# The mixture stages of a four-layer kernel: a tile's down products behind the next tile's up products, rows gathered seven tiles ahead

## The chip, the cores and the metric

The kernel runs on one core of one Trainium2 chip, as one program and one launch. The metric is the time of one execution on the device in microseconds (us); the median of three runs is compared. TensorE is called PE in the profile, VectorE DVE, ScalarE ACT, GpSimd POOL and SyncE SP.

## The reference

The input `x` is 4 sequences of 512 rows of 512 floats (2,048 tokens). Four steps follow one another, each added to `x`: a small cross attention, a feed-forward block 0 (self attention, then a mixture of experts), a second cross attention with a mask, and a feed-forward block 1 (a mixture only). The two mixtures are what the change touches:

```python
# block 0: 1 shared expert and 7 routed ones, inner width 256, each token takes 2
h = silu(x @ wg) * (x @ wu) / 8.0
out = h @ wd                      # summed over the chosen experts with their weights
# block 1: 32 routed experts, inner width 192, each token takes 8
h = silu(x @ wg[e]) * (x @ wu[e])
acc = acc + (h @ wd[e]) * w_e[:, None]
```

## The kernel before, in words

All matmuls are float32 in accuracy. The large ones are made of three products in the faster format fp32r: a factor is split into a high part (rounded) and a low part (the rest), and high by high, high by low and low by high are summed.

The function `mixture` runs once for each mixture. The (token, expert) pairs are sorted by expert into tiles of 128 rows; every tile has one expert. Mixture 0 has 56 tiles (the first 16 are those of the shared expert, whose rows come in order by plain DMA), mixture 1 has 160. The tiles are unrolled in groups of 8 (`GROUP`): the first group or groups as straight code, then a hardware loop, then the last group. The engines each run their own list and meet at semaphores; nothing plans the order but the order in which the lines stand. For tile t:

- POOL gathers the 128 rows of the tile from HBM with an indirect DMA (`gather`, L1462) into one of 8 buffers, 6 tiles ahead (`AHEAD`), and later adds the tile's 128 result rows into one of two sums in HBM (`add`, L1478, an indirect DMA that adds). One `gather(t + AHEAD)` and one `add(t)` alternate. An `add` waits for the tile's result, and for the `add` of two tiles before to have landed, since that one wrote the same sum. In mixture 0's shared tiles `keep` (L1469) stands for `add`.
- PE turns the rows (`flip`, L1739, four 128x128 transposes). ACT copies the turned rows to their high part (`flip` of ACT, L1507), DVE makes the low part (`rows_rest`, L1648).
- ACT and DVE split the expert's weights 4 and 3 tiles ahead: ACT the high part of the up weights (`split`, L1524) and of the last rows of the down weights (`tail_of_weights`, L1540), DVE the low parts (`split_rest`, L1654; `tail_rest`, L1668, or `part_rest` L1661 in mixture 0).
- PE runs the up products (`up`, L1758 to L1760, 12 matmuls of 384 columns in mixture 1, of 512 in mixture 0).
- ACT takes the silu (`silu`, L1546), DVE multiplies (`product`, L1676 and L1677) and so makes `hid`.
- PE turns `hid` (L1774, two transposes, called the hidden flip below). ACT (`tail_of_hidden` L1534, `half_of_hidden` L1529) and DVE (`flip` of DVE, L1639 and L1642, or L1636 and L1637) copy it out.
- PE runs the down products (L1784, a float32 matmul that the trace shows as two, then L1789 and L1790, or L1792 to L1794).
- ACT scales the result by the row's weight into one of 4 buffers (L1574), and POOL adds it.

The order of PE in a turn of the loop for tile t is: hidden flip of t, `flip` of t + 2, `up` of t + 1, down products of t. That of ACT: `tail_of_hidden(t)`, `flip(t + 2)`, `expert_of` and `tail_of_weights(t + 4)`, `silu(t + 1)`, `split(t + 4)`, result of t. That of DVE: `flip(t)`, `place_of(t + 3)`, `rows_rest(t + 2)`, `tail_rest(t + 3)`, `product(t + 1)`, `split_rest(t + 3)`.

`expert_of` and `place_of` read a tile's expert from a table in SBUF into a register of the engine, which then forms addresses with it:

```python
needed = act.value_load(of_tile[0:1, 1, bass.ds(t, 1)], min_val=1, max_val=E)
```

SP loads the weights of the experts into a ring of 4, waiting until the down products of the expert four before are done. `listing` turns the table of row numbers once, at the start of a mixture.

## Time and profile before

| what | value |
| --- | --- |
| median of 3 runs (lowest, highest) | 1813.72 us (1808.09, 1817.69) |
| span of the profiled execution, first to last instruction | 1822.5 us |
| PE busy | 1582.2 us, 87% |
| PE weight loads | 1206.6 us, 66% |
| DVE busy | 1399.5 us, 77% |
| ACT busy | 1082.6 us, 59% |
| POOL busy | 789.0 us, 43% |
| the core's granted TensorE clock, mean | 0.913 |

The span is the profiled execution's own time; no other time was taken of that execution. It is 8.8 us (0.5%) above the median of the runs. Mixture 0 lies between about 599 and 907 us, mixture 1 between about 1067 and 1789 us. An engine's busy time is the union of its instructions. Matmuls are pipelined and their ends are modelled, so PE can show no gap and yet wait a little: the starts of its instructions tell more than its idle time.

### The profile page before, as it was taken

The page shows a single profiled execution, that of the slowest core. Times are in us where ns is not written, and L with a number is a line of the kernel's source. Part 1 is how long each engine was busy: PE and PEld are TensorE (multiplying, and loading weights), DVE is VectorE, ACT ScalarE, POOL GpSimd, SP SyncE. Part 2 cuts the span into 40 slices and gives each one's busy share as a digit, 9 for nine tenths or more (in the row PEclk, how much of TensorE's full clock was granted, in tenths as well). Part 3 has the DMA queues.
Part 4 walks back from the last instruction along what each step waited for, and adds up shares of the span by engine and source line. Part 5 has one row for each costly group of instructions (what it writes and reads, how often), then busy time and mean ns, then how long its engine had stood idle before and what let it go on. Part 6 is the DMA issues. An engine that isn't in the chain of part 4 may idle for free. (4 is left out here: it accounts for less than half of the span.)

```text
span 1822.5 us, 34829 instructions
## 1 busy us (share of the span) xinstructions
PE 1582.2 (87%) x8910; PEld 1206.6 (66%) x8911; DVE 1399.5 (77%) x2889; ACT 1082.6 (59%) x2081; POOL 789.0 (43%) x547
## 2 busy tenths in 40 slices
PE   4578899898887799999779929999999999999991
PEld 2546667666565577777546517887878787887880
DVE  6836866767674588888567858998989998998992
ACT  1124634546352477888433317888878887888870
POOL 5100010110302324555301135788878877778881
PEclk9588998999998799999976658999999999999995
DMA  9225436453521635865564415878788888997778
GB/s 338 80 69 133 101 82 150 89 140 74 124 63 47 203 101 135 210 107 107 74 216 139 154 35 132 210 155 202 156 209 170 176 189 198 223 227 164 131 123 301
DMA packets 169999, 270.58 MB, mean 148 GB/s; under 512 B 20416, under 2 KB 96192, under 8 KB 168192
## 3 DMA queue, kind: packets, MB, share of 16 engines
q0 software_dynamic: 49008, 117.24, 32.6%
q1 hardware_dynamic: 120896, 152.18, 28.4%
q8 instruction: 46, 0.75, 0.2%
q14 instruction: 49, 0.40, 0.1%
HBM read 153.72 MB, written 89.06 MB: 133 GB/s over the span
## 5 line engine op out<-in xcount | busy, mean ns | idle before, releaser
L1654 DVE TENSOR_TENSOR moe_w_lo<-moe_w_up,moe_w_hi 128x1536 fp32r<-128x1536 f32 (+1 forms) x216 | 408.6, 1892 | 1.7 <-ACT moe_w_hi L1524 1.7
L1524 ACT ACTIVATE moe_w_hi<-moe_w_up 128x1536 fp32r (+3 forms) x216 | 343.2, 1589 | 0.0
L1462 POOL DMA_INDIRECT moe_rows<-moe_rows,moe_ids x200 | 308.4, 1542 | 67.2 <-issue 57.3
L1758 PE MATMUL psum<-moe_w_hi,moe_rows_hi 128*128 128x384 f32 (+1 forms) x864 | 324.2, 375 | 4.8 <-DVE moe_rows_lo L1648 4.8
L1759 PE MATMUL psum<-moe_w_lo,moe_rows_hi 128*128 128x384 f32 (+1 forms) x864 | 305.5, 354 | 0.0
L1760 PE MATMUL psum<-moe_w_hi,moe_rows_lo 128*128 128x384 f32 (+1 forms) x864 | 305.5, 354 | 0.0
L1784 PE MATMUL psum<-moe_w_down,moe_hid_t 128*128 (+1 forms) x432 | 221.0, 593 | 2.7 <-DVE moe_hid_lo L1637 1.4
L1478 POOL DMA_INDIRECT moe_sum<-moe_res,moe_ids x100 | 172.0, 1720 | 98.3 <-ACT moe_res L1574 49.2
L1478 POOL DMA_INDIRECT moe_other<-moe_res,moe_ids x100 | 172.3, 1723 | 91.7 <-ACT moe_res L1574 30.0
L1648 DVE TENSOR_TENSOR moe_rows_lo<-psum,moe_rows_hi 128x512 fp32r<-128x512 f32 x216 | 149.3, 691 | 69.2 <-issue 53.4
L739 ACT ACTIVATE prob<-psum,neg_top 128x128 f32<-128x128 f32 (+3 forms) x256 | 133.3, 528 | 83.1 <-DVE neg_top L869 78.5
L1758 PEld LDWEIGHTS psum<-moe_w_hi,moe_rows_hi 128*128 128x128 f32 x864 | 165.0, 191 | 13.2 <-DVE moe_rows_lo L1648 5.8
L1760 PEld LDWEIGHTS psum<-moe_w_hi,moe_rows_lo 128*128 128x128 f32 x864 | 164.4, 190 | 9.9
L1759 PEld LDWEIGHTS psum<-moe_w_lo,moe_rows_hi 128*128 128x128 f32 x864 | 165.4, 191 | 7.6
L869 DVE TENSOR_REDUCE neg_top<-psum 128x1 f32<-128x128 f32 (+3 forms) x256 | 117.6, 484 | 50.0 <-PE psum L1093 49.7
L1507 ACT ACTIVATE moe_rows_hi<-psum 128x512 fp32r<-128x512 f32 x216 | 130.6, 605 | 28.5 <-PE psum L1739 28.2
L1739 PE MATMUL psum<-const_sb,moe_rows 128*128 128x128 f32 x864 | 132.1, 276 | 14.1 <-DMA moe_rows<-moe_rows,moe_ids 12.6
L1546 ACT ACTIVATE moe_gate<-psum 128x192 f32<-128x192 f32 (+1 forms) x216 | 74.0, 342 | 110.4 <-PE psum L1760 108.9
L1540 ACT ACTIVATE moe_tail_hi<-moe_w_down 128x512 fp32r (+1 forms) x160 | 101.1, 632 | 61.3 <-issue 57.6
L1134 PE MATMUL psum<-const_sb,prob 128*128 128x128 f32 x640 | 111.3, 290 | 29.8 <-ACT prob L739 26.6
L1789 PE MATMUL psum<-moe_tail_hi,moe_tail_t 128*128 128x512 f32 x160 | 127.2, 795 | 0.0
L293 POOL DMA_INDIRECT moe_slots<-entry,slot x24 | 23.9, 994 | 232.1 <-DVE slot L992 225.6
(295 smaller groups left out, 3121.2 us busy)
## 6 DMA issues: line engine op xcount, KB each, us to landing
moe_w_up<-in_L_ffn_w_gate SPq DMA_DIRECT2D x32, 384.0 KB, 4.5
moe_w_up<-in_L_ffn_w_up SPq DMA_DIRECT2D x32, 384.0 KB, 5.5
q_st<-q_hi SPq DMA_DIRECT2D x64, 128.0 KB, 3.0
k_st<-k_hi SPq DMA_DIRECT2D x64, 128.0 KB, 3.0
k_st<-k_lo SPq DMA_DIRECT2D x64, 128.0 KB, 3.3
q_st<-q_lo SPq DMA_DIRECT2D x64, 128.0 KB, 3.1
moe_w_down<-in_L_ffn_w_down SPq DMA_DIRECT2D x32, 256.0 KB, 6.1
moe_w_down<-in_L_ffn_w_down SPq DMA_DIRECT2D x64, 128.0 KB, 6.5
```

The source lines that it names most:

```text
L739: sc.activation(prob[:, u, e, 0:(i + 1) * P], score_at(n, e, (i + 1) * P), ACT.Exp, bias=neg_top[:, u, e:e + 1], accum_out=den[:, i, 2 * h ...
L1462: pool.indirect_dma_start(rows[u][:, :], None, d["rows"], bass.IndirectOffsetOnAxis(ids[:, t:t + 1], 0)).then_inc(gathered[u], 16)
L1478: pool.indirect_dma_start(sums[t % 2], bass.IndirectOffsetOnAxis(ids[:, t:t + 1], 0), res[t % RESULTS][:, :], None, compute_op=ALU.add).th ...
L1507: sc.activation(rows_hi[i][:, :], ps[:, i, :], ACT.Copy).then_inc(T["rth"], 1)
L1524: sc.activation(w_hi[u % SPLITS][:, :], w_up[:, bass.ds(at * DC, DC), :].rearrange("p a n -> p (a n)"), ACT.Copy).then_inc(T["wh"], 1)
L1648: v.tensor_tensor(rows_lo[i][:, :], ps[:, i, :], rows_hi[i][:, :].bitcast(F32), ALU.subtract).then_inc(T["rts"], 1)
L1654: v.tensor_tensor(w_lo[u % SPLITS][:, :], w_up[:, bass.ds(at * DC, DC), :].rearrange("p a n -> p (a n)"), w_hi[u % SPLITS][:, :].bitcast(F ...
L1739: last = tr(ps[:, i, k * P:(k + 1) * P], rows[u][:, k * P:(k + 1) * P], ident)
L1758: mm(ps[:, 2 + i, 0:2 * I], hi, w_h, start=(k == 0), stop=False)
L1759: mm(ps[:, 2 + i, 0:2 * I], hi, w_l, start=False, stop=False)
L1760: last = mm(ps[:, 2 + i, 0:2 * I], lo, w_h, start=False, stop=(k == DC - 1))
L1784: done = mm(ps[:, 5 + i, :], hid_t[i][:, j, :], tile_at(w_down, at * n_fc + j), start=(j == 0), stop=False)
```

## The change

`AHEAD` goes from 6 to 7. PE's turn for tile t becomes: `flip` of t + 2, `up` of t + 1, hidden flip of t, down products of t - 1 (`down`, new as a function), and then the register load for the next turn. ACT's turn becomes `flip(t + 2)`, `silu(t + 1)`, `tail_of_hidden(t)`, `expert_of` and `tail_of_weights(t + 4)`, `split(t + 4)`, result of t - 1. DVE's turn becomes `rows_rest(t + 2)`, `product(t + 1)`, `flip(t)`, `place_of(t + 3)`, `tail_rest(t + 3)`, `split_rest(t + 3)`. The first turn has no down products, the last has two. The number of instructions of each kind stays what it was. PE's `listing` of mixture 0 moves from turn 3 to turn 4. The program is otherwise the same. The diff, with comments and blank context cut:

```diff
--- before.py
+++ after.py
@@ -35,7 +35,7 @@
 GROUP = 8
 SPLITS = 4
 RESULTS = 4
-AHEAD = 6
+AHEAD = 7
 
 
 QUERY_ORDER = (1, 0, 3, 2)
@@ -1545,33 +1545,39 @@
                 tiles_done(act, "hidden", t - 1)
                 sc.activation(gate[i][:, :], ps[:, 2 + i, 0:I], ACT.Silu).then_inc(T["silu"], 1)
 
+            def result(g, u):
+                i, t = u % 2, g * GROUP + u
+                if moe.runs:
+                    expert = D if isinstance(t, int) and t < KNOWN else \
+                        D - 1 + act.value_load(of_tile[0:1, 1, bass.ds(t, 1)], min_val=1, max_val=E)
+                act.wait_ge(S["down"], t + 1)
+                since(act, emptied[u % RESULTS], emptied_0 + 16 * (g * (GROUP // RESULTS) + u // RESULTS))
+                if moe.runs:
+                    of_row = rows[u][:, bass.ds(expert, 1)]
+                else:
+                    of_row = 1.0 / moe.scaling if isinstance(t, int) and t < SHARED else weight[:, bass.ds(t, 1)]
+                sc.activation(res[u % RESULTS][:, :], ps[:, 5 + i, :], ACT.Copy, scale=of_row).then_inc(T["res"], 1)
+
             def tiles(g, last):
                 for u in range(GROUP):
-                    i, t = u % 2, g * GROUP + u
+                    t = g * GROUP + u
+                    if not last or u < GROUP - 2:
+                        flip(t + 2, u)
+                    if not last or u < GROUP - 1:
+                        silu(t + 1, u + 1)
                     if moe.tail:
                         tail_of_hidden(t, u)
                     else:
                         half_of_hidden(t, u)
-                    if not last or u < GROUP - 2:
-                        flip(t + 2, u)
                     if not last or u < GROUP - SPLITS:
                         at, needed = expert_of(t + SPLITS)
                         if moe.tail:
                             tail_of_weights(t + SPLITS, u + SPLITS, at, needed)
-                    if not last or u < GROUP - 1:
-                        silu(t + 1, u + 1)
-                    if not last or u < GROUP - SPLITS:
                         split(t + SPLITS, u + SPLITS, at, needed)
-                    if moe.runs:
-                        expert = D if isinstance(t, int) and t < KNOWN else \
-                            D - 1 + act.value_load(of_tile[0:1, 1, bass.ds(t, 1)], min_val=1, max_val=E)
-                    act.wait_ge(S["down"], t + 1)
-                    since(act, emptied[u % RESULTS], emptied_0 + 16 * (g * (GROUP // RESULTS) + u // RESULTS))
-                    if moe.runs:
-                        of_row = rows[u][:, bass.ds(expert, 1)]
-                    else:
-                        of_row = 1.0 / moe.scaling if isinstance(t, int) and t < SHARED else weight[:, bass.ds(t, 1)]
-                    sc.activation(res[u % RESULTS][:, :], ps[:, 5 + i, :], ACT.Copy, scale=of_row).then_inc(T["res"], 1)
+                    if not isinstance(t, int) or t > 0:
+                        result(g if u > 0 else g - 1, (u - 1) % GROUP)
+                if last:
+                    result(g, GROUP - 1)
 
             sc.activation(gate[0][:, 0:1], m["ones"][:, 0:1], ACT.Silu)
             for t in range(SPLITS):
@@ -1679,18 +1685,16 @@
             def tiles(g, last):
                 for u in range(GROUP):
                     t = g * GROUP + u
+                    if not last or u < GROUP - 2:
+                        rows_rest(t + 2, u)
+                    if not last or u < GROUP - 1:
+                        product(t + 1, u + 1)
                     flip(t, u)
                     if SHARED and isinstance(t, int) and t == LISTED_AT:
                         listing()
                     if not last or u < GROUP - 3:
                         at = place_of(t + 3)
-                    if not last or u < GROUP - 2:
-                        rows_rest(t + 2, u)
-                    if not last or u < GROUP - 3:
                         (tail_rest if moe.tail else part_rest)(t + 3, u + 3, at)
-                    if not last or u < GROUP - 1:
-                        product(t + 1, u + 1)
-                    if not last or u < GROUP - 3:
                         split_rest(t + 3, u + 3, at)
 
             def place_of(t):
@@ -1740,10 +1744,10 @@
                 last.then_inc(T["rt"], 1)
 
             def place_of(t):
+                if isinstance(t, int) and t == KNOWN - 1:
+                    pe.wait_ge(S["listed"], 1)
                 if isinstance(t, int) and t < KNOWN:
                     return 0
-                if isinstance(t, int) and t == KNOWN:
-                    pe.wait_ge(S["listed"], 1)
                 return pe.value_load(of_tile[0:1, 0, bass.ds(t, 1)], min_val=0, max_val=RING - 1)
 
             def up(g, u):
@@ -1760,40 +1764,49 @@
                     last = mm(ps[:, 2 + i, 0:2 * I], lo, w_h, start=False, stop=(k == DC - 1))
                 last.then_inc(T["up"], 1)
 
+            def down(t, u, at):
+                i, u = u % 2, u % GROUP
+                tiles_done(pe, "hts", t + 1)
+                tiles_done(pe, "res", t - 1)
+                for j in range(n_fc - 1):
+                    mm(ps[:, 5 + i, :], hid_t[i][:, j, :], tile_at(w_down, at * n_fc + j), start=(j == 0), stop=False)
+                if moe.tail:
+                    pe.wait_ge(tail_made["lo"], t + 1)
+                    mm(ps[:, 5 + i, :], tail_t[i][:, :], tail_hi[u][:, :], start=False, stop=False)
+                    done = mm(ps[:, 5 + i, :], tail_t[i][:, :], tail_lo[u][:, :], start=False, stop=True)
+                else:
+                    mm(ps[:, 5 + i, :], hid_hi[i][:, :], part_hi[u][:, :], start=False, stop=False)
+                    mm(ps[:, 5 + i, :], hid_hi[i][:, :], part_lo[u][:, :], start=False, stop=False)
+                    done = mm(ps[:, 5 + i, :], hid_lo[i][:, :], part_hi[u][:, :], start=False, stop=True)
+                done.then_inc(S["down"], 1)
+
+            def hidden_flip(t, u):
+                i = u % 2
+                tiles_done(pe, "hidden", t + 1)
+                tiles_done(pe, "hts", t)
+                for j in range(n_fc):
+                    at_tail = moe.tail and j == n_fc - 1
+                    done = tr(ps[:, 7, 0:P] if at_tail else ps[:, 4, j * P:(j + 1) * P], hid[i][:, j * P:(j + 1) * P], ident)
+                done.then_inc(T["ht"], 1)
+
             def tiles(g, last):
-                at = place_of(g * GROUP)
+                started = isinstance(g, int) and g == 0
+                at = None if started else place_of(g * GROUP - 1)
                 for u in range(GROUP):
-                    i, t = u % 2, g * GROUP + u
+                    t = g * GROUP + u
                     more, over = divmod(u + 1, GROUP)
-                    if not last or u < GROUP - 1:
-                        at_next = place_of(t + 1)
-                    tiles_done(pe, "hidden", t + 1)
-                    tiles_done(pe, "hts", t)
-                    for j in range(n_fc):
-                        at_tail = moe.tail and j == n_fc - 1
-                        done = tr(ps[:, 7, 0:P] if at_tail else ps[:, 4, j * P:(j + 1) * P], hid[i][:, j * P:(j + 1) * P], ident)
-                    done.then_inc(T["ht"], 1)
                     if not last or u < GROUP - 2:
                         flip(g + (u + 2) // GROUP, (u + 2) % GROUP)
                     if not last or u < GROUP - 1:
                         up(g + more, over)
-                    tiles_done(pe, "hts", t + 1)
-                    tiles_done(pe, "res", t - 1)
-                    whole = n_fc - 1
-                    for j in range(whole):
-                        done = mm(ps[:, 5 + i, :], hid_t[i][:, j, :], tile_at(w_down, at * n_fc + j), start=(j == 0), stop=False)
-                    if SHARED and isinstance(t, int) and t == LISTED_AT - 1:
+                    hidden_flip(t, u)
+                    if SHARED and isinstance(t, int) and t == LISTED_AT:
                         listing()
-                    if moe.tail:
-                        pe.wait_ge(tail_made["lo"], t + 1)
-                        mm(ps[:, 5 + i, :], tail_t[i][:, :], tail_hi[u][:, :], start=False, stop=False)
-                        done = mm(ps[:, 5 + i, :], tail_t[i][:, :], tail_lo[u][:, :], start=False, stop=True)
-                    else:
-                        mm(ps[:, 5 + i, :], hid_hi[i][:, :], part_hi[u][:, :], start=False, stop=False)
-                        mm(ps[:, 5 + i, :], hid_hi[i][:, :], part_lo[u][:, :], start=False, stop=False)
-                        done = mm(ps[:, 5 + i, :], hid_lo[i][:, :], part_hi[u][:, :], start=False, stop=True)
-                    done.then_inc(S["down"], 1)
-                    at = at_next
+                    if not started or u > 0:
+                        down(t - 1, u - 1, at)
+                    at = place_of(t)
+                if last:
+                    down(N - 1, GROUP - 1, at)
 
             if not SHARED:
                 listing()
```

## Rows read from the trace of the kernel before

**Rows 1.** Windows: PE, PEld, DVE, ACT, POOL busy, TensorE clock, DMA share, GB/s.
```profile
700.00:800.00 100.00, 100.00 (x462) 75.70 (x461) 86.15 (x121) 80.04 (x121) 52.19 (x40) 1.00 0.73 166
...
1300.00:1400.00 100.00, 94.98 (x501) 77.09 (x500) 88.71 (x160) 82.09 (x138) 78.78 (x46) 1.00 0.84 188
```

**Rows 2.** Groups by line, 1150 to 1700 us: busy us, mean ns.
```profile
L1784 PE MATMUL psum<-moe_w_down,moe_hid_t 128*128 x256 | 130.6, 592 | 0.0
```

**Rows 3.** Timeline of PE, two tiles of mixture 1: start, duration.
```profile
1302.16 0.42 PE L1758 MATMUL psum<-moe_w_hi,moe_rows_hi 128*128 128x384 f32 x1
...
1306.57 0.42 PE L1758 MATMUL psum<-moe_w_hi,moe_rows_hi 128*128 128x384 f32 x1
...
1308.73 1.02 PE L1784 MATMUL psum<-moe_w_down,moe_hid_t 128*128 x2
...
1310.05 0.39 PE L1774 MATMUL psum<-const_sb,moe_hid 128*128 128x128 f32 x2
...
1310.64 0.42 PE L1758 MATMUL psum<-moe_w_hi,moe_rows_hi 128*128 128x384 f32 x1
```

**Rows 4.** Waits, 1150 to 1700 us: total, times, longest.
```profile
ACT moe_tail_hi L1540 <- issue: 44.9, 85, 0.9
...
DVE moe_rows_lo L1648 <- issue: 32.8, 86, 1.0
...
POOL moe_other L1478 <- DMA moe_other<-moe_res,moe_ids: 21.3, 13, 2.7
PEld psum L1774 <- DVE moe_hid L1677: 20.9, 62, 0.7
...
PE psum L1739 <- DMA moe_rows<-moe_rows,moe_ids: 10.5, 11, 2.1
...
POOL moe_sum L1478 <- ACT moe_res L1574: 4.3, 2, 3.5
```

**Rows 5.** Timeline of DVE and ACT in the same tiles.
```profile
1305.35 1.75 DVE L1654 TENSOR_TENSOR moe_w_lo<-moe_w_up,moe_w_hi 128x1536 fp32r<-128x1536 f32 x1
...
1306.12 0.69 ACT L1574 ACTIVATE moe_res<-psum,moe_rows 128x512 f32<-128x512 f32 x1
...
1308.14 0.69 DVE L1648 TENSOR_TENSOR moe_rows_lo<-psum,moe_rows_hi 128x512 fp32r<-128x512 f32 x1 [0.54 <-issue]
...
1309.01 0.33 ACT L1546 ACTIVATE moe_gate<-psum 128x192 f32<-128x192 f32 x1
```

**Rows 6.** Timeline of POOL in the same tiles.
```profile
1306.20 1.76 POOL L1462 DMA_INDIRECT moe_rows<-moe_rows,moe_ids  x1 [0.31 <-issue]
1309.98 3.11 POOL L1478 DMA_INDIRECT moe_sum<-moe_res,moe_ids  x1 [2.02 <-DMA moe_sum<-moe_res,moe_ids]
```

**Rows 7.** Timeline at mixture 1's start, POOL and DVE.
```profile
1095.32 2.23 POOL L1462 DMA_INDIRECT moe_rows<-moe_rows,moe_ids  x1 [0.30 <-issue]
...
1096.64 0.68 DVE L1668 TENSOR_TENSOR moe_tail_lo<-moe_w_down,moe_tail_hi 128x512 fp32r<-128x512 f32 x1
1097.24 0.69 DVE L1648 TENSOR_TENSOR moe_rows_lo<-psum,moe_rows_hi 128x512 fp32r<-128x512 f32 x1
```

**Rows 8.** Timeline of PE: first hidden flip of mixture 0 and of 1.
```profile
621.34 0.44 PE L1774 MATMUL psum<-const_sb,moe_hid 128*128 128x128 f32 x2 [1.92 <-DVE moe_hid L1677]
...
1100.64 0.69 PE L1774 MATMUL psum<-const_sb,moe_hid 128*128 128x128 f32 x2 [3.54 <-DVE moe_hid L1677]
```

**Rows 9.** Timeline at both ends: the last down products, POOL's last adds.
```profile
899.64 1.12 PE L1784 MATMUL psum<-moe_w_down,moe_hid_t 128*128 x2 [1.45 <-DVE moe_hid_lo L1637]
...
1778.63 1.55 POOL L1478 DMA_INDIRECT moe_other<-moe_res,moe_ids  x1 [1.77 <-DMA moe_other<-moe_res,moe_ids]
...
1781.37 1.12 PE L1784 MATMUL psum<-moe_w_down,moe_hid_t 128*128 x2 [1.26 <-DVE moe_tail_t L1642]
...
1784.06 1.55 POOL L1478 DMA_INDIRECT moe_other<-moe_res,moe_ids  x1 [1.41 <-ACT moe_res L1574]
1789.33 0.35 SPq L2249 DMA_DIRECT2D e_one<-moe_sum  x1
```

## Prediction

> **What bounds the kernel now.** I read the windows first. In mixture 0 PE is busy 100.00 of 100 us at the full granted clock, DVE 86, ACT 80, POOL 52. In mixture 1 nothing stands out so: PE 95, DVE 89, ACT 82, POOL 79, the DMA engines 0.84 of the time, clock 1.00 [rows 1]. A share of the time doesn't say which wait ends last, so the next view is the starts of PE's instructions, tile by tile.
>
> The groups by line count 256 halves of the float32 down matmul in 550 us, so 128 tiles of 550/128 = 4.30 us each [rows 2]. The timeline has a tile that takes 1310.64 - 1306.57 = 4.07 us, with no wait that matters: 2.16 us of up products, 1.32 of down products, 0.59 of the two flips. I take 4.07 as PE's floor. The tile before it took 1306.57 - 1302.16 = 4.41 us [rows 3]. So PE loses 0.23 us a tile in mixture 1, 29 us in these 550. In mixture 0 I take nothing as lost, since PE shows no gap there.
>
> The waits say where the 29 us go [rows 4]. PE waited for gathered rows 10.5 us in 11 stalls. Ends of matmuls are modelled and overlap the next start, so I count some 0.2 us more for each: 13 us. The weight load of the hidden flip waited for the product 20.9 us in 62 times; it overlaps matmuls still running, so less of it costs time. The tile of 4.41 us is the first of a group of 8, where two register loads stand behind one another. One in eight tiles loses 0.34 us so: 16 x 0.3 = 5 us. That leaves 29 - 13 - 5 = 11 us for hidden flips that come late.
>
> Why they are late is in ACT and DVE: 44.9 us before L1540 and 32.8 us before L1648 are "issue", in 85 and 86 of 128 tiles [rows 4]. In the timeline DVE stands still 0.54 us there [rows 5], just where the code has the register load of `place_of`. When the load is slow, the product behind it is late for a flip that has only 1.32 us of down products before it.
>
> POOL has its own story. It waited 21.3 us for an earlier add to land, in one of the two sums alone, and hardly for results (4.3 us) [rows 4]: in mixture 1 it runs behind, and its lateness shows as PE's stalls for rows.
>
> **The change part by part.** PE's order. The hidden flip of t moves behind `flip` and `up` of t + 1's turn of PE, the down products behind the hidden flip of the next tile. Cover for the silu and the product grows from 1.32 us (down) to 1.32 + 0.36 + 2.16 = 3.8 us. So the 11 us in this stretch go if nothing new is late. For the whole stage, 160 tiles, that would be 14; its last tiles and first ones wait less. I take -9 us, ends 0 and -14. The double register load at a group's turn stays, now between down products and rows' flip: 0. In mixture 0 the steady tiles have no wait to lose: 0.
>
> What could be late next is rows' high part. ACT's turn now starts with `flip`, and its two following steps wait for PE's up products and hidden flip. Its work is 0.82 x 4.30 = 3.5 us a tile [rows 1]. The silu starts 2.44 us after the up products start (1309.01 - 1306.57) [rows 3, 5]. The register load then has only `tail_of_hidden` before it as cover; I give it an exposed 0.6 us, near the issue time above (44.9/85 = 0.53). So the result, with all of ACT's other work but `flip` before it (3.5 - 0.6 - 0.5 = 2.4), starts at 2.44 + 2.4 + 0.6 = 5.4 us, and the rows' high part ends at 5.4 + 0.6 + 0.5 = 6.5 us. DVE needs 0.7 more: 7.2. The up products that read it start two turns after, at 8.14. Margin 0.9 us. The cycle of ACT is 3.5 + 0.6 = 4.1 us only if the load can't be hidden; it starts at PE's hidden flip, however late ACT itself is, so a late ACT catches up. DVE's work is 0.89 x 4.30 = 3.8 us [rows 1], below 4.07. I take 0, and keep a wait of 0.2 us a tile (32 us) as the bad end.
>
> POOL and `AHEAD`. Results used to start 0.45 us before a turn's up products (1306.12 against 1306.57) [rows 3, 5]; now they start 5.4 us after, so 5.85 us later. One tile more ahead gives back 4.07. The gathers lose 1.8 us of their lead. POOL is not waiting for results now, so its own lateness can shrink instead, and the loss is paid about once: +2, and +1 for a shorter tile on the same DMA load: +3 us, ends -5 (lateness that settles lower) and +25. `gather` reuses the buffer of tile t - 1 at t + 7, whose result is then done: no new wait.
>
> The starts. At mixture 1's start the first hidden flip waited 3.54 us, in mixture 0 1.92 us [rows 8]. Now `flip` and `up` of tile 1 stand there instead, and their inputs are ready: DVE ends the low part of tile 1's rows at 1097.93 [rows 7]. The next up products again find DVE busy, so I take -5 of the 5.5 us, ends 0 and -7.
>
> The ends. The last down products waited 1.45 and 1.26 us for the copies of `hid`; now those of the tile before stand there: -2.7. But the last three results leave PE only 1.4 us apart, and the last add waits for the one two before it, which wrote the same sum. That one used to start at 1778.63, and the last landing took from 1784.06 to about 1789.33, 5.3 us [rows 9]. The last up products ended at 1781.37 - 1.32 - 0.3 - 1.4 = 1778.4, and the last add started 5.7 us after them. Now they end 1.3 us sooner, the add two before the last starts some 2.6 us after them (down products, result, POOL's issue), and the last one 2.6 + 5.3 = 7.9 us after them: 0.9 us later than before, for each mixture. I take +2, ends -2.7 and +5. PE's `listing` a turn later: nobody needs it before tile 12.
>
> Seams. Up to hidden flip, hidden flip to down, down to rows' flip are new neighbours on PE; the same matmuls run. 0, ends +-0.03 x 216 = +-6 us.
>
> Sum: -9 + 3 - 5 + 2 = -9 us, against the 1822.5 us of the profiled execution and, since nothing in it hangs on the run, against the median of the runs: 1813.7 - 9 = 1805 us.
>
> **The port between DVE and POOL.** A gather that started at 1306.20, while DVE split weights until 1307.10, took 1.76 us and ended 0.86 after the split [rows 5, 6]. So POOL gets one gather and one add a tile, in step with DVE. In the new order `tail_rest` and `split_rest` stand back to back (0.68 and 1.75 us) with no product between. By the Trainium skill (SBUF — State Buffer, "SBUF: two separate sides"), the pair of ports is locked for a whole instruction when a DVE instruction has two inputs in SBUF, and GpSimd then blocks fully; the trace agrees on that gather. Read strictly, it would shut POOL out of 2.4 us of 4.07 at one go, and the third rival below would be the forecast. Against it: the gather at 1095.32 ended at 1097.55, though `tail_rest` ran from 1096.64 to 1097.32 behind a split [rows 7]. It got in between the two.
>
> **The rivals.**
> 1. The gathers keep the beat. POOL and its adds are the true bound of mixture 1; every us that PE no longer waits for the product it waits for rows. Speaks for it: POOL hardly waits for results, and the DMA engines are at 0.84 [rows 1, 4]. Against: POOL works in step with DVE's splits, so a faster DVE speeds it too. Steady gain of 9 lost: 1805 + 9 = 1814 us.
> 2. Lateness settles lower. Fewer jolts, and half or more of the 13 us of row stalls go too, with -13 instead of -9 for the flips: 1805 - 3 - 4 - 6 = 1792 us.
> 3. POOL is pushed back. An add that waits for a landing does so for 21.3/13 = 1.6 us [rows 4]. It would else start 0.86 + 0.3 = 1.16 us after a split; the block of `tail_rest` and `split_rest` begins 4.07 - 1.75 - 0.68 = 1.64 us after it. So from a wait of 0.5 us on, POOL would stand behind the block, and each late gather comes one split later. 11 stalls in 550 us are 14 in the stage; 14 x 1.75 = 25 us: 1813.7 - 9 + 25 - 3 = 1827 us, slower. A wait for rows' high part at ACT, 0.2 us a tile, would end near the same.
>
> **How the numbers follow.** A measurement of this kernel tells about 0.5% (9 us) from no change: the three runs spread by 9.6 us. The forecast case has 0.48, its own range 1799 to 1811 us, half of it faster by more than 0.5%. Rival 1 has 0.20, rival 2 0.17, rival 3 0.15. Faster: 0.24 + 0.17 + 0.01 (of rival 1) = 0.42. Within 0.5%: 0.24 + 0.17 + 0.03 = 0.44. Slower: 0.02 + 0.12 = 0.14. The range of 8 in 10 reaches from rival 2 to near rival 3: 1791 to 1822 us.
>
> **What the profile after would show.** Right: no PEld wait of the hidden flip for `moe_hid` to speak of, where it was 20.9 us; tiles of 4.07 us in long rows; mixture 0 unchanged at its pace; the first hidden flips without a wait. PE's wait for gathered rows stays near 10.5 us in the same number of tiles. Wrong: that row grows past 20 us (rival 1 or 3; for 3 POOL's mean gather also grows), or up products wait for `moe_rows_lo`, or ACT shows long idle time before L1540. The prediction fails most easily on the row stalls, which I can bound only loosely.

## The result and the profile after

The changed kernel takes 1795.74 us (median of 20 runs, 1780.30 to 1805.13); the kernel before, on the same chips, 1811.57 us (20 runs, 1802.76 to 1818.66). The ratio is 0.9916 [0.9896, 0.9935], so 15 us less, between 12 and 19. The forecast was 9 us less, and 1805 us. The forecast case's own range, 1799 to 1811 us, was 3 to 15 us less, so the measured difference stands at its end.

The profiled execution after has a span of 1783.4 us against 1822.5. Most of that difference of 39 us is not the change's. From POOL's last add of mixture 0 to its first gather of mixture 1, where no line was changed, the one takes 1087.81 - 902.45 = 185.4 us and the other 1069.36 - 896.28 = 173.1 us; the two executions stand at opposite ends of their kernels' spread. I compare stretches inside the mixtures. These differ from one execution to the next too, as the table below shows.

Windows of the kernel after, to be read against [rows 1] (PE, PEld, DVE, ACT, POOL busy, TensorE clock, DMA share, GB/s):

```profile
700.00:800.00 100.00, 100.00 (x463) 75.41 (x462) 86.74 (x121) 81.14 (x121) 53.08 (x40) 1.00 0.72 166
1300.00:1400.00 100.00, 98.00 (x516) 81.82 (x514) 91.71 (x163) 81.12 (x142) 82.63 (x49) 0.98 0.89 196
1400.00:1500.00 100.00, 100.00 (x538) 83.78 (x537) 95.86 (x173) 84.06 (x147) 81.54 (x50) 1.00 0.87 196
```

Mixture 0 has its old pace. In mixture 1 PE is nearly always busy, POOL and the DMA engines are a little busier (over 1200 to 1600 us POOL 325 us after and 319 before, DMA share 0.87 and 0.85). PE's tiles were 4.30 us [rows 2]; after, in 550 us of the same stage (groups by line, 1130 to 1680 us), 265 halves are 132.5 tiles of 4.15 us:

```profile
L1772 PE MATMUL psum<-moe_w_down,moe_hid_t 128*128 x265 | 135.7, 593 | 0.0
```

The waits of the kernel after in the same stretch (total, times, longest), to be read against [rows 4]:

```profile
ACT moe_tail_hi L1540 <- issue: 57.3, 94, 0.9
...
ACT moe_tail_hi L1540 <- PE psum L1776: 25.9, 32, 1.3
...
POOL moe_other L1478 <- DMA moe_other<-moe_res,moe_ids: 12.2, 11, 1.6
POOL moe_sum L1478 <- DMA moe_sum<-moe_res,moe_ids: 10.0, 6, 2.9
PE psum L1743 <- DMA moe_rows<-moe_rows,moe_ids: 4.0, 4, 2.0
...
PEld psum L1743 <- DVE moe_rows_lo L1654: 1.8, 5, 0.6
...
PEld psum L1762 <- DVE moe_rows_lo L1654: 0.4, 2, 0.2
```

There is no row left of the hidden flip waiting for `moe_hid` (20.9 us in 62 before). PE waited for gathered rows 4.0 us in 4 stalls; it was 10.5 in 11. POOL waited less for landings: 12.2 us against 21.3 in the sum `other`, and 10.0 against 13.7 in the other sum, whose waits the prediction left out ("in one of the two sums alone"). ACT is idle longer before L1540 (57.3 + 25.9 us, where "issue" was 44.9). The prediction had this on its list of signs of being wrong; it was none, for hardly anybody waits for it: the one row is DVE's, 0.6 us in 1.

PE's timeline after has this, the first tile of a group of 8 (from 1272.74; the one that took 4.41 us before [rows 3] has the same place, the group's first) and the tile after it, which meets one of the four stalls:

```profile
1272.74 0.42 PE L1762 MATMUL psum<-moe_w_hi,moe_rows_hi 128*128 128x384 f32 x1
...
1276.48 0.60 PE L1743 MATMUL psum<-const_sb,moe_rows 128*128 128x128 f32 x4
1276.84 0.42 PE L1762 MATMUL psum<-moe_w_hi,moe_rows_hi 128*128 128x384 f32 x1
...
1281.68 0.66 PE L1743 MATMUL psum<-const_sb,moe_rows 128*128 128x128 f32 x4 [0.95 <-DMA moe_rows<-moe_rows,moe_ids]
1282.10 0.42 PE L1762 MATMUL psum<-moe_w_hi,moe_rows_hi 128*128 128x384 f32 x1
```

The group's first tile takes 1276.84 - 1272.74 = 4.10 us, as any other: the 0.3 us that it lost before are gone. The stall, marked 0.95, makes its tile 5.26 us, 1.2 more than the others, so the mark understates it by 0.2 as I had assumed.

The starts that the table below rests on are those of the up products of tile 0, tile 4 and the last tile of mixture 1. PE's timeline after:

```profile
1075.13 0.69 PE L1762 MATMUL psum<-moe_w_hi,moe_rows_hi 128*128 128x384 f32 x1
...
1091.43 0.42 PE L1762 MATMUL psum<-moe_w_hi,moe_rows_hi 128*128 128x384 f32 x1
...
1734.38 0.34 PE L1762 MATMUL psum<-moe_w_hi,moe_rows_hi 128*128 128x384 f32 x1
```

and the same three before:

```profile
1093.31 0.69 PE L1758 MATMUL psum<-moe_w_hi,moe_rows_hi 128*128 128x384 f32 x1
...
1116.33 0.42 PE L1758 MATMUL psum<-moe_w_hi,moe_rows_hi 128*128 128x384 f32 x1
...
1776.22 0.42 PE L1758 MATMUL psum<-moe_w_hi,moe_rows_hi 128*128 128x384 f32 x1
```

The first four turns took 1116.33 - 1093.31 = 23.0 us before and 1091.43 - 1075.13 = 16.3 us after. The next 155 tiles took (1776.22 - 1116.33)/155 = 4.257 us each, and (1734.38 - 1091.43)/155 = 4.148 after, which is 17 us for them all in this pair of executions.

### The profile page after: what moved, and what is told of

The parts are those of the page before. It is cut to its first block and busy times, and to the rows that moved or that the text cites. A ratio compares the mean times of both kernels' runs of the same rounds, so it can differ in the third digit from the quotient of the medians.

```text
span 1783.4 us, 34938 instructions
## 1 busy us (share of the span) xinstructions
PE 1558.9 (87%) x8910; PEld 1198.6 (67%) x8911; DVE 1411.2 (79%) x2889; ACT 1071.2 (60%) x2081; POOL 788.0 (44%) x547
## 5 line engine op out<-in xcount | busy, mean ns | idle before, releaser
L1462 POOL DMA_INDIRECT moe_rows<-moe_rows,moe_ids x200 | 293.4, 1467 | 67.5 <-issue 57.0
L1478 POOL DMA_INDIRECT moe_sum<-moe_res,moe_ids x100 | 179.2, 1792 | 85.6 <-ACT moe_res L1559 40.0
L1478 POOL DMA_INDIRECT moe_other<-moe_res,moe_ids x100 | 179.9, 1799 | 81.2 <-ACT moe_res L1559 23.6
L1762 PEld LDWEIGHTS psum<-moe_w_hi,moe_rows_hi 128*128 128x128 f32 x864 | 164.2, 190 | 13.8 <-DVE moe_rows_lo L1654 5.7
L1654 DVE TENSOR_TENSOR moe_rows_lo<-psum,moe_rows_hi 128x512 fp32r<-128x512 f32 x216 | 149.2, 691 | 23.8 <-ACT moe_rows_hi L1507 13.5
L1540 ACT ACTIVATE moe_tail_hi<-moe_w_down 128x512 fp32r (+1 forms) x160 | 101.1, 632 | 100.2 <-issue 71.5
L1507 ACT ACTIVATE moe_rows_hi<-psum 128x512 fp32r<-128x512 f32 x216 | 126.9, 588 | 22.7 <-PE psum L1743 22.7
L1743 PEld LDWEIGHTS psum<-const_sb,moe_rows 128*128 128x128 f32 x864 | 107.1, 141 | 43.2 <-DMA moe_rows<-moe_rows,moe_ids 7.8
```

The lines of the kernel that those rows point to most:

```text
L1462: pool.indirect_dma_start(rows[u][:, :], None, d["rows"], bass.IndirectOffsetOnAxis(ids[:, t:t + 1], 0)).then_inc(gathered[u], 16)
L1478: pool.indirect_dma_start(sums[t % 2], bass.IndirectOffsetOnAxis(ids[:, t:t + 1], 0), res[t % RESULTS][:, :], None, compute_op=ALU.add).th ...
L1654: v.tensor_tensor(rows_lo[i][:, :], ps[:, i, :], rows_hi[i][:, :].bitcast(F32), ALU.subtract).then_inc(T["rts"], 1)
L1743: last = tr(ps[:, i, k * P:(k + 1) * P], rows[u][:, k * P:(k + 1) * P], ident)
L1762: mm(ps[:, 2 + i, 0:2 * I], hi, w_h, start=(k == 0), stop=False)
```

## The experiments

Each kernel was timed in five rounds against the kernel before on the same chip; its one profiled execution gives the last two columns, read as above (that of order_in_mix1 isn't compared). "Pace" is us a tile over the last 155 tiles of mixture 1, "first four" the time of the first four turns there. Each is from one execution, and the pace of the old order alone ranges from 4.193 to 4.288 below, so a difference of 0.05 between two rows says nothing.

| kernel | orders, `AHEAD` | ratio [95%] | pace | first four |
| --- | --- | --- | --- | --- |
| before | old, 6 | 1 | 4.257 | 23.0 |
| ahead7_alone | old, 7 | 1.0023 [0.9993, 1.0053] | 4.271 | 21.8 |
| before_early_loads | old, 6 | 1.0006 [0.9958, 1.0055] | 4.240 | 21.9 |
| before_busy_start | old, 6 | 1.0011 [0.9974, 1.0049] | 4.193 | 20.0 |
| before_plain_writes | old, 6 | 0.9909 [0.9875, 0.9943] | 4.140 | 21.7 |
| order_in_mix0 | new in mixture 0 alone, 7 | 1.0011 [0.9980, 1.0041] | 4.288 | 21.8 |
| order_in_mix1 | new in mixture 1 alone, 7 | 0.9912 [0.9875, 0.9949] | | |
| pe_order_alone | PE's new, the others' old, 7 | 1.0341 [1.0288, 1.0393] | 4.513 | 19.9 |
| order_ahead6 | new, 6 | 0.9964 [0.9930, 0.9998] | 4.237 | 16.3 |
| after | new, 7 | 0.9916 [0.9896, 0.9935] | 4.148 | 16.3 |
| order_ahead8 | new, 8 | 0.9944 [0.9912, 0.9975] | 4.134 | 16.3 |
| order_tail_apart | new, DVE's pair apart, 7 | 0.9916 [0.9877, 0.9956] | 4.203 | 16.2 |
| order_early_loads | new, 7 | 0.9898 [0.9862, 0.9934] | 4.167 | 16.1 |
| order_plain_writes | new, 7 | 0.9874 [0.9833, 0.9915] | 4.127 | 16.3 |

### The two parts apart: ahead7_alone, order_ahead6

```diff
 # ahead7_alone, against before
-AHEAD = 6
+AHEAD = 7
 # order_ahead6, against after
-AHEAD = 7
+AHEAD = 6
```

> Rows gathered seven tiles ahead, all orders as before. If the gain of the change is in its orders (cover for the hidden flip, fuller starts), this is within 5 us of before: ratio 0.997 to 1.002, with PE's wait for gathered rows at most some us smaller than 10.5 in 550 us, and the hidden flip's weight load still waiting some 20 us. If the gain is in the lead of the gathers, it shows here alone: ratio about 0.993, row stalls near 0.

> The new orders, rows still gathered six tiles ahead: the lead shrinks by 5.8 us against before. If the lead is what row stalls hang on, PE waits for rows several times as long as in the changed kernel and a good part of the gain goes: ratio 0.995 to 1.01. If POOL's lateness only settles where PE's stalls allow it (my step 'paid about once'), it costs about 4 to 6 us against the changed kernel: ratio 0.994 to 0.996.

Seven tiles ahead alone gains nothing. Its waits (1150 to 1700 us) show why:

```profile
PEld psum L1774 <- DVE moe_hid L1677: 18.9, 40, 1.0
...
ACT moe_res L1574 <- DMA moe_sum<-moe_res,moe_ids: 13.1, 12, 1.9
PE psum L1774 <- DVE moe_hid L1677: 10.2, 18, 0.9
ACT moe_res L1574 <- DMA moe_other<-moe_res,moe_ids: 9.6, 7, 1.7
```

PE's wait for rows is gone altogether, and in its place ACT waits 22.7 us for a result buffer whose add has not landed, and PE waits for the product behind that. Late adds show at the gathers with 6 ahead and at the buffers with 7: the lateness was moved.

The new orders with 6 ahead gain 0.4%, half of what they gain with 7. Here PE does wait for rows:

```profile
PE psum L1743 <- DMA moe_rows<-moe_rows,moe_ids: 16.6, 13, 2.1
```

So neither part has the gain. In order_ahead6 the gathers lost lead to the later results, as the forecast said (POOL now waits for results 63.9 us in 62, 5.0 us in 4 before); with one more tile ahead, the new order does not pay at the buffers what the old order paid.

### The two mixtures apart: order_in_mix1, order_in_mix0

```diff
+        LATE_DOWN = moe is MOE1       # MOE0 in order_in_mix0
...
-            groups(act, tiles)
+            groups(act, tiles if LATE_DOWN else tiles_old)
...
-            groups(dve, tiles)
+            groups(dve, tiles if LATE_DOWN else tiles_old)
...
-            groups(pe, tiles)
+            groups(pe, tiles if LATE_DOWN else tiles_old)
```

> New orders in mixture 1 alone, seven tiles ahead in both. By the forecast's steps the steady gain (9 us), the start of mixture 1 (3.5 us, after the two traces rather 5) and its end are here: -9 to -13 us, ratio 0.993 to 0.995. If mixture 0 had the larger part, the ratio is above 0.997.

> New orders in mixture 0 alone. By the forecast's steps only its start (1.9 us, after the two traces rather 4) less its end (+1) is here: -1 to -4 us, ratio 0.998 to 1.000, with tiles of 4.99 us as before. If the new neighbours on PE save or cost something in each tile it shows here purely: 0.03 us a tile is 1.7 us.

The gain is mixture 1's (0.9912). In mixture 0 alone nothing can be told from no change, though its first four turns took 18.3 us in place of 22 to 24: less than 3 us net stay under the 0.3% that these rounds resolve. Its tiles keep their 5.00 us, so the new neighbours on PE cost nothing there.

### The register loads: before_early_loads, order_early_loads

The prediction put the late hidden flips down to slow register loads on ACT and DVE. Here both are issued a turn sooner, so that nothing stands right behind them:

```diff
 # DVE; ACT's expert_of likewise
             def tiles(g, last):
+                at = place_of(g * GROUP + 3)
                 for u in range(GROUP):
...
-                    if not last or u < GROUP - 3:
-                        at = place_of(t + 3)
...
                         split_rest(t + 3, u + 3, at)
+                    if u < GROUP - 1 and (not last or u < GROUP - 4):
+                        at = place_of(t + 4)
```

> The kernel before, with the register loads of ACT and DVE made a turn earlier, behind the long weight splits, so that no load stands ahead of the product. If late hidden flips come from slow register loads (my step), their wait (20.9 us in 550) falls to about a third, the issue time before L1540 and L1648 goes, and the kernel is 5 to 9 us faster: ratio 0.995 to 0.997. If lateness of POOL and its adds is the true bound of mixture 1, the waits go and the time doesn't: 0.999 to 1.001, with more wait for rows.

> The changed kernel with the register loads of ACT and DVE a turn earlier. With the hidden flip covered there is nothing late for them to mend: same as the change, 0.990 to 0.993, though ACT's issue time before L1540 (57 us in 550) goes. If ACT's turn was near its limit for PE (rows' high part), it is faster by 3 us or more: below 0.990.

The waits of before_early_loads, 1150 to 1700 us:

```profile
PEld psum L1777 <- DVE moe_hid L1679: 9.6, 28, 0.6
...
PE psum L1742 <- DMA moe_rows<-moe_rows,moe_ids: 9.5, 13, 1.7
```

The hidden flip's wait halved (20.9 to 9.6 us), and the 32.8 us of "issue" before DVE's rows are nearly gone (2.4 us), as are the 44.9 before ACT's L1540. The time is the same, 1.0006. That is less proof than it looks. The interval reaches down to 0.9958, so a gain of up to 8 us, most of what was forecast, isn't excluded. And the edit moved the idle time more than it removed it, for ACT now has it in other places:

```profile
ACT moe_res L1576 <- issue: 11.5, 25, 0.6
ACT moe_gate L1546 <- issue: 11.3, 20, 1.0
```

The copy L1534 has 9.4 us more. By the starts of the up products, the second tiles of the groups lose 3.6 us in all, where they lost 1.3 before. So the loads made the wait seen in [rows 4], and half of that wait could go without a gain that shows; that the loads cost nothing is not shown. On the new order the same edit gives 0.9898, within the interval of the change alone, with no "issue" row before L1540 left (57.3 us in the change).

### PE's order without the others': pe_order_alone

```diff
 # ACT and DVE, against after: the old order of their steps, but result(t - 1) stays
-                    if not last or u < GROUP - 2:
-                        rows_rest(t + 2, u)
-                    if not last or u < GROUP - 1:
-                        product(t + 1, u + 1)
                     flip(t, u)
...
```

> PE's new order and the result of t - 1, seven tiles ahead, but ACT and DVE in their old order (tail_of_hidden and flip of t first). If the other engines' orders matter, they now wait at each turn for a hidden flip that comes 2.5 us later, the rows' high part is late for the up products and each tile of mixture 1 takes 0.5 to 1.5 us more: ratio 1.03 or above. If their orders don't matter, 0.992 as the change.

Its waits, 1150 to 1700 us:

```profile
ACT moe_tail_t L1534 <- PE psum L1792: 51.0, 89, 0.8
...
PEld psum L1765 <- DVE moe_rows_lo L1655: 38.1, 98, 0.6
```

With the copies of the hidden flip first in their turn, ACT and DVE stand waiting for a flip that PE now makes at the turn's end, and the rows behind them come late for the up products: 3.4% slower. Every tile of both mixtures is longer, by some 0.25 us (4.51 in mixture 1, 5.25 in mixture 0), and not by the 0.5 to 1.5 expected. PE's order can't be changed alone; the new orders of ACT and DVE without PE's were not tried.

### The clock at the start: before_busy_start

```diff
             up(0, 0)
+            keep_busy(nc, m, c, 3, 6)
             groups(pe, tiles)
```

> The kernel before, with three idle products of PE (results not used) in the wait before the first hidden flip of each mixture. If the start gains more than its wait because PE's clock rises sooner, tiles 1 to 4 of mixture 1 run sooner at the full clock and the first four turns take 1 to 3 us less in the trace. If the start's gain is only the wait, they take as long or longer. The whole time can't tell: 0.998 to 1.001.

Windows at the start of mixture 1 (columns as above). In the kernel before, whose first up products start at 1093.31:

```profile
1097.00:1101.00 4.00, 0.46 (x3) 0.36 (x3) 3.59 (x6) 2.19 (x4) 0.55 (x1) 0.86 0.29 87
1101.00:1105.00 4.00, 4.00 (x16) 4.00 (x15) 1.88 (x4) 1.51 (x3) 0.00 (x0) 0.50 0.00 0
1105.00:1109.00 4.00, 4.00 (x19) 3.11 (x18) 2.56 (x5) 2.91 (x5) 0.24 (x1) 0.79 0.00 0
```

In before_busy_start, where they start at 1094.81:

```profile
1098.80:1102.80 4.00, 2.82 (x12) 1.38 (x11) 3.45 (x7) 2.02 (x4) 0.10 (x1) 1.00 0.27 70
1102.80:1106.80 4.00, 4.00 (x24) 3.39 (x23) 3.01 (x6) 3.04 (x5) 0.00 (x0) 1.00 0.00 0
```

In the kernel after, where they start at 1075.13:

```profile
1075.00:1079.00 4.00, 4.00 (x14) 3.87 (x13) 2.29 (x3) 4.00 (x6) 3.39 (x3) 0.50 0.72 214
1079.00:1083.00 4.00, 3.66 (x22) 3.23 (x21) 4.00 (x8) 2.85 (x6) 1.32 (x2) 0.89 0.54 139
1083.00:1087.00 4.00, 4.00 (x24) 3.35 (x23) 3.73 (x8) 3.42 (x7) 0.00 (x0) 1.00 0.00 0
```

Before, PE idled through the wait for the product (busy 0.46 of 4 us), and the next up products ran at a granted clock of 0.50, the 1.2 GHz level. With filler matmuls in the wait they ran at 1.00 (2.4 GHz). After, the wait is filled by tile 1's own flip and up products, and the clock is 0.89 and then 1.00. The first four turns of before_busy_start took 20.0 us where the old order takes 21.8 to 23.0. The second turn alone, the one right behind the wait, took 4.05 us for 5.1 to 6.3; the rest is in the first turn, which differs between executions of the old order too (8.0 to 8.6 us). So the clock is worth 1 to 2 us there by the second turn, and up to 3 by all four. In mixture 0 the filler gained nothing (22.8 us for the first four turns, where the old order takes 22.1 to 23.6). In the kernel's time it can't be told from nothing (1.0011).

### Port contention: order_tail_apart

```diff
                         product(t + 1, u + 1)
+                    if not last or u < GROUP - 3:
+                        at = place_of(t + 3)
+                        (tail_rest if moe.tail else part_rest)(t + 3, u + 3, at)
                     flip(t, u)
...
-                    if not last or u < GROUP - 3:
-                        at = place_of(t + 3)
-                        (tail_rest if moe.tail else part_rest)(t + 3, u + 3, at)
                         split_rest(t + 3, u + 3, at)
```

> The changed kernel, with DVE's tail_rest moved ahead of its flip, so that the two instructions that shut POOL out stand 0.6 us apart. If the block of both back to back pushes POOL back (rival 3), the mean gather and the row stalls fall and it is faster than the change: 0.988 or below. If POOL gets in between the two anyway, no difference: 0.991 to 0.993. The load of place_of now stands before the copies of the hidden flip, which have 2 us of slack.

The ratio is that of the change to the fourth digit. POOL's groups in it, 1150 to 1700 us (count, busy us, mean ns of one):

```profile
L1462 POOL DMA_INDIRECT moe_rows<-moe_rows,moe_ids x130 | 170.3, 1310 | 39.6 <-issue 33.5 <-ACT moe_res L1559 5.2 <-DMA moe_other<-moe_res,moe_ids 0.6
...
L1478 POOL DMA_INDIRECT moe_sum<-moe_res,moe_ids x66 | 140.6, 2130 | 30.9 <-issue 17.1 <-DMA moe_sum<-moe_res,moe_ids 8.3 <-ACT moe_res L1559 5.5
```

and in the kernel after, 1130 to 1680 us:

```profile
L1462 POOL DMA_INDIRECT moe_rows<-moe_rows,moe_ids x132 | 217.0, 1644 | 40.2 <-issue 36.6 <-ACT moe_res L1559 1.8 <-DMA moe_other<-moe_res,moe_ids 1.2
...
L1478 POOL DMA_INDIRECT moe_sum<-moe_res,moe_ids x66 | 118.0, 1788 | 30.6 <-issue 19.8 <-DMA moe_sum<-moe_res,moe_ids 10.0 <-ACT moe_res L1559 0.8
```

A gather and an add together take 1.31 + 2.13 = 3.44 us with the pair apart and 1.64 + 1.79 = 3.43 with it together. Which of the two is stretched depends on where DVE's long instructions stand; the sum does not. The edit has a price of its own: the weight load of `flip` now waits for `moe_rows_lo` 6.5 us in 8 (1.8 in 5 in the change), and the first tiles of the groups take 4.25 us (median) for 4.10. So a gain by the port could hide behind that price and the interval (7 us to either side). But the row stalls, where rival 3 put its cost, are no smaller by anything that shows (4.7 us, 5.3 in the change, by the table further down).

### What the adds cost: before_plain_writes, order_plain_writes

```diff
-                pool.indirect_dma_start(sums[t % 2], bass.IndirectOffsetOnAxis(ids[:, t:t + 1], 0), res[t % RESULTS][:, :], None,
-                                        compute_op=ALU.add).then_inc(emptied[t % RESULTS], 16)
+                pool.indirect_dma_start(sums[t % 2], bass.IndirectOffsetOnAxis(ids[:, t:t + 1], 0), res[t % RESULTS][:, :], None).then_inc(emptied[t % RESULTS], 16)
```

> The kernel before, but the result rows are written over the sums instead of added to them (the sums are then wrong: each token keeps one expert's part). The DMA engines no longer read the old rows and each write lands sooner. If the row stalls of mixture 1 come from adds that land late, they go: -10 to -14 us, ratio 0.992 to 0.994, and what is left of PE's loss are the late hidden flips. If they come from POOL's own instructions, the time stays: 0.998 to 1.001.

> The changed kernel with the same plain writes. Against the run above this is the change without late adds: if the cover for the hidden flip is the gain, it stays at 9 to 14 us below it with its starts (ratio to before about 0.984); if the change gains by what it does to gathers and adds, the two come out within 6 us of one another.

Without the addition in the DMA, the old order is as fast as the change (0.9909), and the change gains on top only 0.9874/0.9909 = 0.9965, 6 us, with intervals that overlap. In before_plain_writes, groups by line and waits, 1150 to 1700 us:

```profile
L1462 POOL DMA_INDIRECT moe_rows<-moe_rows,moe_ids x133 | 132.3, 995 | 40.6 <-issue 40.3 <-DMA moe_other<-moe_res,moe_ids 0.3
```

```profile
POOL moe_sum L1478 <- ACT moe_res L1573: 121.6, 63, 2.5
...
DVE moe_rows_lo L1647 <- issue: 21.3, 97, 0.4
...
PEld psum L1773 <- DVE moe_hid L1676: 9.3, 39, 0.4
...
ACT moe_tail_hi L1539 <- issue: 6.2, 20, 0.4
```

POOL's gathers take 1.0 us (1.67 before), POOL waits for results (232.9 us in all) and hardly for landings (9.5 us in 5), and no row says that PE waits for gathered rows. The DMA engines are busy 0.63 of 1200 to 1600 us, where they were 0.85. So the old order lost its time in mixture 1 to the adds more than to its own length: with plain writes it has neither row stalls nor, but for the first tiles of the groups, late hidden flips (1.4 us in all, 9.3 before).

What about the adds cost the time is not separated. The edit makes them land sooner, it shortens POOL's own instruction (1.78 to 0.99 us, so the condition of the second case isn't met), and it shortens the idle time that stands where the register loads are: the "issue" before ACT's L1539 and DVE's L1647 is 6.2 + 21.3 us, none longer than 0.4, where it was 44.9 + 32.8 with some of 0.9 and 1.0 [rows 4]. The gathers are shorter for another reason: POOL, waiting for results, now begins them outside DVE's split (see the rivals, below).

### One tile further: order_ahead8

```diff
-AHEAD = 7
+AHEAD = 8
```

> The changed kernel with rows gathered eight tiles ahead, which is one for each buffer: the gather of t + 8 has to wait for the result of t. POOL lags behind results anyway, so if the lead is what the row stalls hang on they shrink further (14 to 20 us above the floor become 8 to 12): ratio 0.987 to 0.990. If POOL's place in the order counts instead, the gather's new wait for the result delays the add and nothing is gained or some is lost: 0.991 to 0.996.

0.9944 against 0.9916, intervals that overlap; its pace is 4.134 us and ACT begins to wait for result buffers again (4.2 us in 4 and 2.8 us in 4). There is nothing more to have from the lead.

## Why the prediction was right, and where not

The direction was right and the size was not: 15 us [12, 19] for 9. The steady part, by the profiled executions of both orders (the pace of four of the old with the adds as they are, 4.257, 4.271, 4.288, 4.240, and of before_busy_start, 4.193, mean 4.250; of four of the new with 7 or 8 ahead, mean 4.163), gave 155 x 0.087 = 13 us; forecast were 9 - 3 = 6. By the scatter of these nine executions the 13 is sure to some 4 us, an estimate.

Where it was lost and won can be counted by the starts of the up products. The table has what the 155 tiles took above 4.07 us each, in us: tiles in which PE's `flip` waited for rows (how many), the first tiles of the groups, and all others.

| execution | row stalls | first tiles | others | sum |
| --- | --- | --- | --- | --- |
| before | 13.5 (11) | 6.2 | 9.3 | 29.0 |
| before_early_loads | 13.3 (13) | 4.8 | 8.2 | 26.3 |
| before_busy_start | 2.5 (5) | 6.0 | 10.6 | 19.1 |
| after | 5.3 (4) | 3.0 | 3.8 | 12.1 |
| order_ahead8 | 4.2 (5) | 1.9 | 3.9 | 10.0 |
| order_early_loads | 12.1 (9) | 0.4 | 2.6 | 15.1 |
| order_tail_apart | 4.7 (5) | 8.0 | 8.0 | 20.7 |
| order_ahead6 | 21.1 (14) | 0.3 | 4.4 | 25.8 |
| ahead7_alone | 0 | 13.8 | 17.3 | 31.1 |
| before_plain_writes | 0 | 9.5 | 1.4 | 10.9 |
| order_plain_writes | 0 | 1.1 | 7.7 | 8.8 |

**Hidden flips, steady: -9 forecast.** The wait went in full, and this term came out as forecast: the "others" before are nearly all tiles with a late hidden flip, 9.3 us (8.2 and 10.6 in two more executions of the old order). After, the 3.8 us are the seams (below) and no late flip. What made the flips late is less clear than the prediction had it. Slow register loads made most of the wait in the waits' view, but before_early_loads halved that wait without a gain that shows, and with plain writes the late flips went although the order stayed. That leaves the loads, slow beside the adds, or the adds in some other way.

**First tiles of the groups: 0 forecast, -3 to -6 measured.** By the medians over 18 groups they took 4.41 us before and 4.10 after. At the other places it was 4.07 to 4.20 before and 4.09 to 4.11 after. "The double register load at a group's turn stays ... 0" was wrong: both loads are still there, and 18 x 0.3 = 5 to 6 us by the medians, 3 to 4 by the sums, are gone. That PE's queue can read its registers during the down products, since their inputs are ready a turn before, would explain it; that was argued and not tried.

**Row stalls: +3 forecast.** I took the loss of lead as paid and lateness as fixed. Alone, each half was near that: with 6 ahead PE's waits for rows rose from 10.5 to 16.6 us, and 7 ahead in the old order moved the lateness to the result buffers. Together they fell to 4.0 us in 4, -8 in this pair. But the pair flatters: stalls differ from 2.5 to 13.5 us between executions of the old order, and from 4.2 to 12.1 in the new with 7 or 8 ahead. The means are 9.8 (three executions) and 6.6 (four). So the +3 did not come; whether it was -3 or -8 is not settled. The direction is that of rival 2, to which I gave 0.17. Why the new order does not pay at the buffers: its ACT turn ends with the result of t - 1, whose lateness then reaches only `flip`, one turn ahead of need, and not the copies for down products that PE is about to run. That fits the waits; it was not tried by itself.

**ACT's margin.** Forecast: the result starts 5.4 us after a turn's up products, the rows' low part ends at 7.2, its reader starts at 8.14. The timeline of ACT after, with up products at 1396.83 and 1405.03:

```profile
1401.39 1.48 ACT L1524 ACTIVATE moe_w_hi<-moe_w_up 128x1536 fp32r x1
1402.77 0.67 ACT L1559 ACTIVATE moe_res<-psum,moe_rows 128x512 f32<-128x512 f32 x1
1403.33 0.59 ACT L1507 ACTIVATE moe_rows_hi<-psum 128x512 fp32r<-128x512 f32 x1
```

Result at 1402.77 - 1396.83 = 5.9 us, high part done at 7.1; the low part (DVE, 0.69 us) starts at 1403.95 and ends at 7.8; the reader starts at 8.2. The margin is 0.4 us, less than half of the 0.9 I had, and it held: in 132 tiles the weight load of the up products waited for `moe_rows_lo` 0.4 us in 2, and that of the `flip` before them is put down to it 1.8 us in 5.

**Starts: -5 forecast, -7 measured.** In mixture 1 the first four turns fell from 22.1 us (mean of before, ahead7_alone, before_early_loads and order_in_mix0) to 16.2, less the 1.33 us of down products that moved out of them: -4.6. In mixture 0, 614.81 to 638.45 against 611.87 to 630.04, other executions 22.1 to 22.8 against 18.0 to 19.4: about -4.2 + 1.56 = -2.6, where 1.56 us are the down products of mixture 0. The part not forecast is the clock in mixture 1; in mixture 0, where the filler gained nothing, nothing was tried for it.

**Ends: +2 forecast, +2 measured.** POOL's last adds after:

```profile
1739.28 1.55 POOL L1478 DMA_INDIRECT moe_other<-moe_res,moe_ids  x1 [2.04 <-ACT moe_res L1559]
...
1745.15 1.55 POOL L1478 DMA_INDIRECT moe_other<-moe_res,moe_ids  x1 [2.13 <-DMA moe_other<-moe_res,moe_ids]
```

The last add starts 1745.15 - 1734.38 = 10.8 us after the last up products, before 1784.06 - 1776.22 = 7.8 [rows 9]; it waits for the add two before, as forecast. Less the 1.33 us of one more tile's down products that is +1.6; in mixture 0, 896.28 - 884.97 against 902.45 - 893.41, less 1.56, it is +0.7.

**Seams: 0 forecast.** An undisturbed tile of mixture 1 went from 4.07 to 4.10, 155 x 0.03 = 4 to 5 us, within the end of 6 us that I gave. **Mixture 0, steady: 0**, and so it was: window of 700 to 800 us with 463 matmuls where there were 462.

Steady -13, starts -7, ends +2 make -18, where the times say -12 to -19. The range of 8 in 10, 1791 to 1822 us, held. That the error is no more than 6 us is partly luck: the seams' 4 us hid as much of what first tiles, row stalls and starts gave beyond the forecast.

**The rivals.** Rival 1 (the gathers keep the beat): PE's tiles shortened, and POOL kept up with them. With 6 ahead it came half true: there row stalls took 21.1 us, and the time fell by 0.4% only. Its premise, that the adds bound mixture 1, is borne out by the plain writes; what it missed is that order and lead together get round most of it. Rival 3 (POOL pushed back) did not come: the kernel is faster, the row stalls did not rise, and order_tail_apart, with the pair apart, is no better. The pair and two POOL instructions around it in the kernel after:

```profile
1401.00 1.60 POOL L1478 DMA_INDIRECT moe_sum<-moe_res,moe_ids  x1 [0.30 <-issue]
...
1401.49 0.69 DVE L1674 TENSOR_TENSOR moe_tail_lo<-moe_w_down,moe_tail_hi 128x512 fp32r<-128x512 f32 x1
1402.10 1.75 DVE L1660 TENSOR_TENSOR moe_w_lo<-moe_w_up,moe_w_hi 128x1536 fp32r<-128x1536 f32 x1
1402.90 1.81 POOL L1462 DMA_INDIRECT moe_rows<-moe_rows,moe_ids  x1 [0.30 <-issue]
```

The add that began 0.49 us before the pair takes 1.60 us, near the 1.55 of one alone, and ends inside the pair. The gather that began inside the split ends at 1404.71, 0.86 us after it. The timeline of the whole stretch from 1150 to 1680 us says the same: the 81 gathers that began during a split ended 0.85 to 0.87 us after it, and those that began during neither of DVE's two took 0.99 us (median), whether or not one of the two began behind them. The Trainium skill (SBUF — State Buffer, "SBUF: two separate sides") has a DVE instruction with two inputs in SBUF and a GpSimd instruction that reads SBUF share a pair of ports: whichever starts first gets it for its whole instruction, and the other blocks fully. For POOL the trace agrees. For DVE it shows no block: a split that began behind a POOL instruction took its usual 1.75 us (124 times, median). And POOL gets in between DVE's two, as the prediction argued against its third rival: 31 gathers that began during `tail_rest` ended 0.86 us (median) after it, though the split had begun by then.

## What to carry to other kernels

Time that a weight load spends waiting in a trace is not all time lost, since matmuls run meanwhile; count the starts of PE's instructions, grouped by their place in the unrolled loop, before giving the loss a cause, and do so in more than one execution. When a late transfer shows at one buffer, more lead moves it to the next buffer in the ring: judge lead and order together, since here lead alone gained nothing, order alone half, and both together all of it. To move one engine's work behind the next tile's, move the other engines' steps too: PE's order alone cost 3.4%.

## What the runs showed of the hardware

An indirect DMA that adds 128 rows of 2 KB into HBM costs more than one that writes them. With plain writes in the old order POOL's own instruction went from 1.78 us to 0.99 (mean), the DMA engines' share from 0.85 to 0.63, the median landing from 6.0 and 5.6 us to 2.8 and 2.9, and the kernel's time fell by 0.9%. That is as much as the new order gains; 10 to 14 us were expected, and it was 16.5.

A gather takes 0.99 us when it begins clear of DVE's long instructions with two inputs in SBUF, and ends 0.86 us after the end of a split when it begins during it, while DVE's split takes 1.75 us either way (kernel after). The mean of 1.67 us in the kernel before, and of 1.00 with plain writes, is mostly a matter of where the gathers begin: at 1301.99 us, say, in before_plain_writes, behind the split that ended at 1300.81.
